# Two of three exponential steps of a chunk moved from tiles 12 to 17 to tiles 18 to 28 of a two-layer transformer kernel

## The chip, the cores and the metric

The kernel runs on one core of one Trainium2 chip. The metric is the device time of one execution in microseconds (us). The kernel before took 1702.78 us in the median of three runs (1702.22 to 1704.12).

## What is computed

Two layers over 32 sequences of 256 tokens with 128 features. Each layer normalises its rows and adds an attention and a mixture of experts to them, all in fp32:

```
x = x + L0_attn(xn) + L0_ffn(xn)        # xn = layernorm(x)
x = x + L1_attn(xn) + L1_ffn(xn)
# L0_attn: linear attention, 16 heads of 8
q_feat = elu(rope(q) * scale) + 1 ;  k_feat = elu(rope(k)) + 1
kv = k_feat^T v ;  den = q_feat . sum(k_feat) ;  out = (q_feat kv / den) W_out
# L0_ffn: 64 experts (8 of them per token, chosen by groups) and a shared one: silu(x Wg) * (x Wu) * coef, times Wd
# L1_attn: 8 best keys per row, softmax over them, and a local message of 4 neighbours with silu
# L1_ffn: 8 experts, 2 per token, gate = softmax(x gate_w)
```

elu(z) + 1 is computed as exp(min(z, 0)) + max(z, 0).

## The kernel before, in words

The tokens are cut into 16 chunks of 512. Layer 0's experts are 33 tiles of 128 hidden columns (32 pairs of experts and the shared one), so TensorE goes through 16 x 33 = 528 tiles, each with three fp32r products for the gate, three for the up half (`first_products`, lines 719 to 721) and the down product of the tile four before (`last_products`: two fp32 passes, line 779, or three fp32r ones, lines 767 to 770, at every fourth tile). Layer 1's expert units follow as another 90 units.

For each tile g, ScalarE computes silu of the gate product (`silu`, L1423) and VectorE multiplies it by the up product (`times_up`, L1003) and, once for two tiles, by the routing coefficients (`times_coef`, L991). There are two PSUM banks for gate products and two for up products: the gate product of tile g waits for silu(g-2), and its up product for times_up(g-2).

Everything else is done beside these tiles, in an order that is written out by hand. The tables `ATTENTION0`, `ROUTE0`, `ROUTE1`, `ATTENTION1` and others give for every step the tile of the chunk at which it is placed; `make_plan` turns them into one list per tile. Each engine runs its instructions in program order, and at every tile g each engine first issues its part of the tile (silu, times_up, products) and then its part of the steps of `plan[g]`, in the tables' order: ATTENTION0, ROUTE0 of the next chunk, ROUTE1 and ATTENTION1 of the chunk before. A step that has not got its operands blocks all that stands behind it on its engine.

The steps that matter here, with their lines:
- `feat_exp` (ScalarE, L1526 and L1528): exp of `k_low` (in the tile mix_a) and of `tmp0`. `q_feat`: relu on ScalarE (L1531), then the sum on GpSimd (L1657). `k_feat` (VectorE, L1127).
- `kvsum` (TensorE, L856), eight products of the features with the values; it waits for k_feat. `kvmask` (VectorE, L1132 and L1134) reads it out. `num0`, `num1` (TensorE, L864) wait for kvmask and for q_feat. `mix0`, `mix1` (VectorE, L1141 to L1145) divide; `mixT` (TensorE, L734, and a copy on ScalarE) transposes.
- `gate_exp` (ScalarE, L1552): exp of layer 1's gate, 32 columns. `attend_exp` (ScalarE, L1561): exp of layer 1's attention scores, at tile 18.
- `near`, `self` (TensorE, three fp32r products each), `p0`, `p1`, `mixa`, `coefT`, `mixl`: other side products. `add1` to `add4`, `mixa_add` (VectorE, L1302), `choice`, `pair4` ... `weigh`: other steps of VectorE.

All side products share three PSUM banks. `make_plan` gives them out in the order of the steps (`free.pop(0)`), and takes a bank back at the step that reads it (`TAKES`). On the chip the next user of a bank waits until the reader before has really finished (`wait_bank`).

exp, silu and sigmoid lie in different activation tables; where ScalarE goes from one to another, the compiler puts an ACT_TABLE_LOAD ahead of the instruction.

The first chunk has a table of its own (`EARLY0`), and chunk 15 has `ROUTE1_LAST`, whose gate_exp is at tile 12. In the text, G(t) is the start of the third gate product (L721) of tile t of chunk 8, which begins at 721.8 us, and silu(t), mul(t) and coef(t) are silu, times_up and times_coef of tile t.

Of the kernel before, what the change touches and what calls it, by code (L numbers as in the profile page):

```python
# [68 lines left out]


ATTENTION0 = [(1, "keys0"), (2, "k_rope"), (4, "q"), (5, "q_copy"), (6, "k_min"), (8, "q_cos"), (9, "q_sin"), (10, "q_min"),
              (12, "feat_exp"), (13, "q_feat"), (14, "k_feat"), (16, "kvsum"), (17, "kvmask"), (19, "num0"), (20, "num1"), (20, "mix0"),
              (24, "mix1"), (26, "mixT")]
FINISH0 = [(4, "yT"), (5, "y_add")]
ROUTE0 = [(0, "stats0"), (2, "norm0"), (4, "xT0"), (5, "x_lo0"), (8, "vr0"), (8, "vr1"), (9, "score"),
          (18, "choice"), (18, "pair4"), (19, "pair2"), (20, "pair1"), (21, "gtop"), (22, "gstrike"), (23, "groups"), (24, "top8"),
          (25, "strike"), (26, "weigh"), (28, "coefT")]

ROUTE0_SECOND = [(at + 6 if at < 10 else at + 1 if at < 14 else at, what) for at, what in ROUTE0]
ROUTE1 = [(5, "stats1"), (7, "norm1"), (8, "xT1"), (9, "x_lo1"), (10, "vl0"), (10, "vl1"), (11, "top1"), (12, "gate_exp"), (23, "softmax"), (30, "select"),  # L80
          (31, "prefix"), (39, "rank"), (40, "key"), (41, "first2"), (42, "slot"), (43, "send0"), (45, "send1"), (47, "send2"), (48, "send3"),
          (49, "send4"), (51, "send5"), (53, "send6"), (54, "send7")]

# [38 lines left out]
def splits1(c):  # L122

    return SPLITS1_FIRST <= c < SPLITS1_FIRST + PARTS1 // SPLITS1_EACH


def make_plan():
# [11 lines left out]
    for g in range(TILES):  # L139
# [3 lines left out]
        steps += [(ROUTE0 if c > 0 else ROUTE0_SECOND, c + 1)] if c + 1 < CHUNKS else []  # L143
        steps += [(ROUTE1 if c < SPARSE else ROUTE1_LAST, c - 1), (ATTENTION1, c - 1)] if c > 0 else [(PREP1, 0)]
        steps += [(SPLITS1, c)] if splits1(c) else []
        plan[g] += [(what, c - 2) for at, what in ROUTE1 if at == j + TILES0 and c > 1]
        plan[g] += [(what, key) for table, key in steps for at, what in table if at == j]
# [1671 lines left out]
```

## Time and profile before

| | |
|---|---|
| median of the runs | 1702.78 us |
| the profiled execution's own time | 1702.63 us |
| its span | 1700.7 us |
| TensorE matmul | 1668.5 us busy (98%) |
| VectorE | 1377.4 us (81%) |
| ScalarE | 877.6 us (52%) |
| GpSimd | 637.5 us (37%) |
| ACT_TABLE_LOAD on ScalarE | 99 of 1.283 us |
| one chunk of 33 tiles in the middle | 88.3 to 88.8 us |

The profile is of one execution on the chip. PE is TensorE, DVE VectorE, ACT ScalarE, POOL GpSimd. In a timeline a row has the start in us, the time it took, engine, line, operation, what it writes and reads, shapes and count; a bracket at its end is the idle time of the engine before it and what ended it. A matmul's end is modelled, and the first product behind an fp32 one is shown early and long; so the third gate product of a tile is the best mark of where TensorE is.

### The profile page before, as it was taken

Reading aid. Unit: us, or ns where it says so; the run is one execution under the profiler, and the core shown is the slowest. Engines: PE = TensorE matmul, PEld = TensorE weight load, DVE = VectorE, ACT = ScalarE, POOL = GpSimd, SP = SyncE. Lnnn points to the kernel's source line nnn. Section 1 sums busy time; section 2 is a strip of 40 time slices with the busy share of each in tenths; the row PEclk is TensorE's granted clock in tenths of the full one; section 3 lists DMA queues with packets and bytes.
Section 4 is the critical chain, followed back from the end, with each engine's and each line's share of the span. In section 5 each row is a group of like instructions: output and inputs, shape, how many; then the busy total and the mean of one; then the engine's idle time right before and its main releaser. Section 6 shows DMA issues by size and latency. Waiting matters only on the chain.

```text
span 1700.7 us, 25018 instructions
## 1 busy us (share of the span) xinstructions
PE 1668.5 (98%) x7158; PEld 1208.5 (71%) x7158; DVE 1377.4 (81%) x3677; ACT 877.6 (52%) x1582; POOL 637.5 (37%) x637
## 2 busy tenths in 40 slices
PE   6999999999999999999999999999999999999997
PEld 4677777777777777777777777777777776767774
DVE  6868888888989797979798888888888887565557
ACT  5546464646464546464555555454646354554432
POOL 4411342424242424333333232333333243567770
PEclk9999999999999999999999999999999999999999
DMA  8858464646374737373737374655546355677758
GB/s 225 195 126 238 116 186 98 186 112 182 99 184 102 180 104 196 97 202 91 196 90 193 87 183 101 160 124 131 152 100 177 91 123 154 211 261 265 239 174 314
DMA packets 172309, 273.92 MB, mean 161 GB/s; under 512 B 14280, under 2 KB 57288, under 8 KB 171920
## 3 DMA queue, kind: packets, MB, share of 16 engines
q1 hardware_dynamic: 163600, 254.63, 56.3%
q0 software_dynamic: 8576, 17.70, 3.3%
q8 instruction: 61, 1.00, 0.3%
q14 instruction: 72, 0.59, 0.1%
HBM read 202.15 MB, written 65.93 MB: 158 GB/s over the span
## 4 chain that ended last, share of the span: by engine, by line
PE 79%; DVE 9%; ACT 6%; issue 4%; DMA 1%; SPq 0%; DVEq 0%; POOL 0%; ACTq 0%; POOLq 0%
PE ps_y L779 17%; PE ps_up L719 7%; PE ps_up L721 7%; PE ps_up L720 7%; PE ps_gate L719 7%; PE ps_gate L721 7%; PE ps_gate L720 7%; PE ps_y L805 4%; PE ps_side L734 3%; DVE silu_h L1003 2%; ACT L1423 1%; DVE silu_h L991 1%; PE ps_side L828 1%; ACT silu_h L1423 1%; ACT L1526 1%
## 5 line engine op out<-in xcount | busy, mean ns | idle before, releaser
L1003 DVE TENSOR_TENSOR silu_h<-ps_up,silu_h 128x512 f32<-128x512 f32 x618 | 421.4, 684 | 267.2 <-ACT silu_h L1423 202.5
L1423 ACT ACTIVATE silu_h<-ps_gate 128x512 f32<-128x512 f32 x618 | 365.9, 598 | 496.0 <-PE ps_gate L721 491.4
L779 PE MATMUL ps_y<-silu_h,w_dn 128*128 128x512 f32 x800 | 407.8, 591 | 1.3 <-DVE silu_h L991 1.3
L991 DVE TENSOR_TENSOR silu_h<-coef_b,silu_h 128x1024 f32<-128x1024 f32 x256 | 321.4, 1256 | 4.4 <-DMA coef_b<-coef_kept 3.2
L719 PE MATMUL ps_gate<-xnT,w_gu 128*128 128x512 f32 x528 | 307.7, 583 | 0.0
L719 PE MATMUL ps_up<-xnT,w_gu 128*128 128x512 f32 x528 | 212.0, 402 | 4.9 <-DVE silu_h L1003 4.6
L721 PE MATMUL ps_gate<-xnT,w_gu 128*128 128x512 f32 x528 | 209.0, 396 | 0.0
L721 PE MATMUL ps_up<-xnT,w_gu 128*128 128x512 f32 x528 | 207.6, 393 | 0.0
L720 PE MATMUL ps_gate<-xnT,w_gu 128*128 128x512 f32 x528 | 206.9, 392 | 0.0
L720 PE MATMUL ps_up<-xnT,w_gu 128*128 128x512 f32 x528 | 206.8, 392 | 0.0
L1705 POOL TENSOR_TENSOR msg<-msg 128x512 f32<-128x512 f32 x48 | 76.7, 1598 | 315.3 <-ACT msg L1586 315.3
L779 PEld LDWEIGHTS ps_y<-silu_h,w_dn 128*128 128x128 f32 x800 | 150.3, 188 | 42.0 <-issue 8.1
L1699 POOL DMA_INDIRECT slots_x<-rows,slot_of x120 | 134.6, 1122 | 110.4 <-PE ps_gate L721 78.3
L1679 POOL DMA_INDIRECT y_kept<-ys,y_to x148 | 143.8, 971 | 59.8 <-issue 48.9
L720 PEld LDWEIGHTS ps_gate<-xnT,w_gu 128*128 128x128 f32 x528 | 100.5, 190 | 54.7 <-issue 48.0
L719 PEld LDWEIGHTS ps_gate<-xnT,w_gu 128*128 128x128 f32 x528 | 100.2, 190 | 54.8 <-issue 46.4
L1638 POOL TENSOR_TENSOR rstd<-rstd,minus_half 128x4 f32<-128x4 f32 x32 | 43.5, 1359 | 244.3 <-DVE shift L1015 244.3
L719 PEld LDWEIGHTS ps_up<-xnT,w_gu 128*128 128x128 f32 x528 | 99.4, 188 | 41.2 <-DVE silu_h L1003 19.8
L721 PEld LDWEIGHTS ps_up<-xnT,w_gu 128*128 128x128 f32 x528 | 99.2, 188 | 23.0
L721 PEld LDWEIGHTS ps_gate<-xnT,w_gu 128*128 128x128 f32 x528 | 99.5, 188 | 22.5
L720 PEld LDWEIGHTS ps_up<-xnT,w_gu 128*128 128x128 f32 x528 | 99.6, 189 | 20.8
L1386 DVE TENSOR_TENSOR h_lo<-silu_h,h_hi 128x512 fp32r<-128x512 f32 x120 | 107.1, 892 | 0.0
(289 smaller groups left out, 2866.7 us busy)
## 6 DMA issues: line engine op xcount, KB each, us to landing
coef_b<-coef_kept SPq DMA_DIRECT2D x254, 512.0 KB, 6.9
slots_x<-empty SPq DMA_DIRECT2D x15, 2080.0 KB, 12.1
w_block<-w_kept SPq DMA_DIRECT2D x45, 512.0 KB, 4.0
xs<-slots_x SPq DMA_DIRECT2D x37, 260.0 KB, 3.8
y_back<-y_kept SPq DMA_DIRECT2D x15, 512.0 KB, 6.8
w_down<-in_ffn_w SPq DMA_DIRECT2D x45, 128.0 KB, 3.8
w_raw<-in_ffn_w SPq DMA_DIRECT2D x33, 128.0 KB, 5.8
xres<-in_x SPq DMA_DIRECT2D x16, 256.0 KB, 2.9
```

What stands on the lines that cost most here:

```text
L719: eng.matmul(dst, w[0], m[0], start=start, stop=False)
L720: eng.matmul(dst, w[1], m[0], start=False, stop=False)
L721: return eng.matmul(dst, w[0], m[1], start=False, stop=stop)
L779: eng.matmul(ps_y[:, :], down_of(j), silu_h[:, h_at(g)], start=j == 0, stop=last).then_inc(pe_down)
L805: eng.matmul(ps_y[:, :], w_down[:, t % BUFS1, f], silu_h[:, h_at(g)], start=first, stop=last).then_inc(pe_down)
L991: eng.tensor_tensor(silu_h[:, s:s + 2], coef_b[:, q % COEF_RING, k:k + 2], silu_h[:, s:s + 2], ALU.mult).then_inc(dve_h)
L1003: eng.tensor_tensor(silu_h[:, s], ps_up[g % 2][:, :], silu_h[:, s], ALU.mult).then_inc(dve_h1)
L1386: eng.tensor_tensor(h_lo[:, :], silu_h[:, h_at(g)], f32(h_hi[:, :]), ALU.subtract).then_inc(dve_hlo)
L1423: eng.activation(silu_h[:, s], ps_gate[g % 2][:, :], ACT.Silu).then_inc(act_silu)
L1679: eng.indirect_dma_start(y_kept, bass.IndirectOffsetOnAxis(y_to[:, c % XPLACES, r:r + 1], 0), ys[:, c % BUFS1, r], None).then_inc(landed[c ...
L1699: eng.indirect_dma_start(slots_x, bass.IndirectOffsetOnAxis(slot_of[:, c % 2, r, k:k + 1], 0), rows1[:, c % 2, r], None).then_inc(sent[c % ...
L1705: eng.tensor_tensor(msg[:, 0], msg[:, 0], msg[:, 1 + k % 2], ALU.add).then_inc(pool_heard)
```

## The change

Only numbers in two tables change. `feat_exp` goes from tile 12 to 18, `q_feat` from 13 to 19, `k_feat` from 14 to 20, `kvsum` from 16 to 21, `kvmask` from 17 to 22, `num0` from 19 to 23, `num1` and `mix0` from 20 to 24, `mix1` from 24 to 26 and `mixT` from 26 to 28, in chunks 1 to 15. `gate_exp` goes from tile 12 to 18 in chunks 1 to 14. `EARLY0`, `ROUTE1_LAST` and `ROUTE1_DENSE` stay as they are. No instruction of the program text is added or removed; the compiler sets the table loads by the new order, and `make_plan` gives out the side banks anew.

```
-              (12, "feat_exp"), (13, "q_feat"), (14, "k_feat"), (16, "kvsum"), (17, "kvmask"), (19, "num0"), (20, "num1"), (20, "mix0"),
-              (24, "mix1"), (26, "mixT")]
+              (18, "feat_exp"), (19, "q_feat"), (20, "k_feat"), (21, "kvsum"), (22, "kvmask"), (23, "num0"), (24, "num1"), (24, "mix0"),
+              (26, "mix1"), (28, "mixT")]
...
-ROUTE1 = [(5, "stats1"), ... (11, "top1"), (12, "gate_exp"), (23, "softmax"), ...
+ROUTE1 = [(5, "stats1"), ... (11, "top1"), (18, "gate_exp"), (23, "softmax"), ...
```

The side banks of a chunk, by the order of the steps (bank numbers 0 to 2, for chunk 8):

| tile | before | after |
|---|---|---|
| 12, 13 | s0 0, s1 2 | s0 0, s1 1 |
| 16, 19, 20 | kvsum 1, num0 0, num1 2 | none |
| 21 | none | kvsum 2 |
| 23 | p0 1, near 0 | num0 0, p0 1, near 2 |
| 24 | p1 1, self 0 | num1 1, p1 2, self 0 |
| 26 | mixT 2, mixa 1 | mixa 2 |
| 28 | coefT 2 | mixT 1, coefT 2 |
| 32 | mixl 1 | mixl 1 |

## Rows read from the trace of the kernel before

**Rows 1.** The page's part 1: busy time, share and instructions of each engine.

```profile
PE 1668.5 (98%) x7158; PEld 1208.5 (71%) x7158; DVE 1377.4 (81%) x3677; ACT 877.6 (52%) x1582; POOL 637.5 (37%) x637
```

**Rows 2.** Waits of PE, 130 to 1480 us, the longest: us in total, times, longest.

```profile
PE ps_up L719 <- DVE silu_h L1003: 3.7, 16, 1.0
```

**Rows 3.** Groups of ACT, by form: table loads (count, busy us, mean ns).

```profile
L1423 ACT ACT_TABLE_LOAD x49 | 62.9, 1283 | 1.0
...
L1526 ACT ACT_TABLE_LOAD x16 | 20.5, 1283 | 0.3
L1561 ACT ACT_TABLE_LOAD x16 | 20.5, 1283 | 0.3
```

**Rows 4.** Timeline of ACT, chunk 8, tiles 12 and 13.

```profile
757.30 1.28 ACT L1526 ACT_TABLE_LOAD   x1
...
761.18 0.60 ACT L1423 ACTIVATE silu_h<-ps_gate 128x512 f32<-128x512 f32 x1
...
762.18 0.63 ACT L1531 ACTIVATE qf<-qf 128x512 f32<-128x512 f32 x1
```

**Rows 5.** Timeline of DVE, tiles 13 and 14: mul(13), h_lo, mul(14).

```profile
761.81 0.69 DVE L1003 TENSOR_TENSOR silu_h<-ps_up,silu_h 128x512 f32<-128x512 f32 x1 [3.14 <-ACT silu_h L1423]
...
763.07 1.66 DVE L1386 TENSOR_TENSOR h_lo<-silu_h,h_hi 128x512 fp32r<-128x512 f32 x1
...
765.79 0.68 DVE L1003 TENSOR_TENSOR silu_h<-ps_up,silu_h 128x512 f32<-128x512 f32 x1
```

**Rows 6.** Timeline of PE, tile 16: G(16), first up product, kvsum.

```profile
765.94 0.40 PE L721 MATMUL ps_gate<-xnT,w_gu 128*128 128x512 f32 x1
766.52 0.50 PE L719 MATMUL ps_up<-xnT,w_gu 128*128 128x512 f32 x1 [0.18 <-DVE silu_h L1003]
...
768.18 1.05 PE L856 MATMUL ps_side<-v,kf 128*128 128x129 f32 x8
```

**Rows 7.** Timeline of ACT, tiles 18 to 20: silu(18), attend_exp, silu(19) and silu(20).

```profile
772.27 0.60 ACT L1423 ACTIVATE silu_h<-ps_gate 128x512 f32<-128x512 f32 x1 [1.12 <-PE ps_gate L721]
...
774.27 1.50 ACT L1561 ACTIVATE scores<-scores,top_neg 128x128 f32<-128x128 f32 x4
...
777.08 1.09 ACT L1423 ACTIVATE silu_h<-ps_gate 128x512 f32<-128x512 f32 x2
```

**Rows 8.** Timeline of POOL, tile 14: the sum of q_feat.

```profile
762.91 1.28 POOL L1657 TENSOR_TENSOR qf<-qf,tmp 128x512 f32<-128x512 f32 x1 [3.91 <-ACT qf L1531]
```

**Rows 9.** Timeline of DVE: k_feat, kvmask, coef(19), mul(21), mul(22), mul(24), mix1, mixa_add, mul(28).

```profile
766.39 0.68 DVE L1127 SCALAR_TENSOR_TENSOR kf<-kf,mix_a 128x512 f32<-128x512 f32 x1
...
772.67 0.91 DVE L1134 TENSOR_SCALAR kv<-att_const,ps_side 128x16 f32<-128x16 f32 x2
...
778.98 1.22 DVE L991 TENSOR_TENSOR silu_h<-coef_b,silu_h 128x1024 f32<-128x1024 f32 x1
...
782.42 0.68 DVE L1003 TENSOR_TENSOR silu_h<-ps_up,silu_h 128x512 f32<-128x512 f32 x1
...
785.80 0.68 DVE L1003 TENSOR_TENSOR silu_h<-ps_up,silu_h 128x512 f32<-128x512 f32 x1
...
790.43 0.68 DVE L1003 TENSOR_TENSOR silu_h<-ps_up,silu_h 128x512 f32<-128x512 f32 x1
...
791.63 0.42 DVE L1145 TENSOR_TENSOR tmp<-ps_side,den_inv 128x256 f32<-128x256 f32 x1
...
799.92 1.13 DVE L1302 SCALAR_TENSOR_TENSOR xres<-ps_side,psum,xres 128x128 f32<-128x128 f32 x4
...
802.70 0.68 DVE L1003 TENSOR_TENSOR silu_h<-ps_up,silu_h 128x512 f32<-128x512 f32 x1
```

**Rows 10.** Timeline of PE: G(21), G(25) and G(29).

```profile
779.31 0.39 PE L721 MATMUL ps_gate<-xnT,w_gu 128*128 128x512 f32 x1
...
790.14 0.39 PE L721 MATMUL ps_gate<-xnT,w_gu 128*128 128x512 f32 x1
...
800.91 0.40 PE L721 MATMUL ps_gate<-xnT,w_gu 128*128 128x512 f32 x1
```

More of the change, by code:

```diff
@@ L79 @@
 ROUTE0_SECOND = [(at + 6 if at < 10 else at + 1 if at < 14 else at, what) for at, what in ROUTE0]
-ROUTE1 = [(5, "stats1"), (7, "norm1"), (8, "xT1"), (9, "x_lo1"), (10, "vl0"), (10, "vl1"), (11, "top1"), (12, "gate_exp"), (23, "softmax"), (30, "select"),
+ROUTE1 = [(5, "stats1"), (7, "norm1"), (8, "xT1"), (9, "x_lo1"), (10, "vl0"), (10, "vl1"), (11, "top1"), (18, "gate_exp"), (23, "softmax"), (30, "select"),
           (31, "prefix"), (39, "rank"), (40, "key"), (41, "first2"), (42, "slot"), (43, "send0"), (45, "send1"), (47, "send2"), (48, "send3"),
```

## The prediction

> **What bounds the kernel now.** I read the shares first: TensorE is busy for 1668.5 of 1700.7 us [rows 1]. Then its waits: from 130 to 1480 us it is held by one thing worth naming, the up product waiting for mul, 3.7 us in 16 waits [rows 2]. So removed work on another engine is worth only what it takes out of such waits, and a new wait on TensorE is paid in full, since nothing behind it has room to catch up. Then the groups of ScalarE: a load of the activation tables takes 1.283 us, and silu, feat_exp and attend_exp cause 49, 16 and 16 of them [rows 3]. Last, the timelines of chunk 8, tile by tile. They show what the waits hide: VectorE, busy for 81%, runs about three us behind TensorE from tile 18 to 30. It is the second bound, and its order matters as much as its sum.
>
> **What goes.** At tile 12 ScalarE loads the exp tables, does two exponentials and the gate's, and loads silu's again: from 757.30 to silu(13) at 761.18, 3.88 us [rows 4]. In chunks 1 to 14 this excursion disappears, for the loads of attend_exp at tile 18 serve all three. That is 14 x 2 = 28 loads x 1.283 = 35.9 us of ScalarE; chunk 15 keeps its gate_exp at tile 12 and its loads. The excursion makes mul(13) wait 3.14 us, h_lo behind it takes 1.66 us since it starts while GpSimd's sum of q_feat runs (762.91 to 764.19), and mul(14) only ends at 766.47 [rows 5, 8]. The up product of tile 16 starts at 766.52, where 765.94 + 0.23 = 766.17 was due, and its first product runs 0.11 longer after the wait [rows 6]: 0.46 us of TensorE. Without the excursion mul(14) is over near 763.6, and this wait is gone: 14 x 0.46 = 6.4 us to the good. That is all that the saved loads are worth directly.
>
> The Trainium skill (ScalarE: Activation LUTs, What ACT_TABLE_LOAD costs) puts a switch at 1283 ns and a drain of some 1380 ns, 2.66 us in all. By it 28 switches would be 74.5 us of ScalarE; the rows have the 1.283 and an exponential right behind it.
>
> **What comes, at tile 21.** kvsum (0.89 us), num0 and num1 (0.49 each) leave tiles 16, 19 and 20, so TensorE gets to tile 21 sooner: from G(16) = 765.94 through four tiles of 2.23 and one of 2.06 it is at G(21) = 776.92, not 779.31 [rows 6, 10]. ScalarE's silu(18) starts at 770.89 (0.49 behind G(18) = 770.40) and ends near 771.5. Then one load (1.28), the two exponentials (0.53 each), the gate's (0.22), attend_exp (1.50, its operands long there) and the load back (1.30): silu(19) runs from 776.89 to 777.49, about as now [rows 7]. The gate product of tile 21 waits for it: G(21) = 777.49 + 0.05 + 0.46 + 0.11 = 778.11, a stall of 1.2 us.
>
> **kvsum behind k_feat.** VectorE sits idle until silu(19), then does mul(19), pair2, coef(19), mul(20) and k_feat. mul(19) at 777.5 puts coef(19) at 778.8. GpSimd's sum of q_feat now starts 0.73 behind the relu (which starts at 777.39), so at 778.12, and lasts to 779.40. By the 1.66 us row coef(19) (1.22 alone) is held to its end and over at 780.5: mul(20) at 780.4, since two neighbours overlap by some 0.1, k_feat 0.6 later at 781.0 (0.68 long), ended at 781.7 [rows 4, 5, 8, 9]. Tile 21's own products end at G(21) + 1.78 = 779.9. kvsum is queued right there and holds tile 22 with it: 1.9 us. With kvsum, G(22) = 783.1, and mul(21) is at 782.4, as it is now.
>
> **num0 behind kvmask.** Between mul(22) and mul(24) VectorE has 1.16 us more, kvmask (0.41 and 0.91, overlapping). It ends at 785.80 + 0.60 + 1.18 = 787.6. TensorE is through with tile 23 at 787.0, so num0 waits 0.7 us, and p0 and near behind it. G(24) = 789.6.
>
> **self behind mix0.** mul(24) comes at 790.43 + 1.16 = 791.6; mix0 follows it in the place where mix1 is now and ends at 791.6 + 1.62 = 793.2 [rows 9]. By the new order of the side banks self takes bank 0 from num0, which mix0 has to have read (now it takes it from near, which ScalarE copies at once). TensorE is there at 792.2: 1.0 us more, plus 0.11, then self. G(25) = 794.5 instead of 790.14, 4.4 us late [rows 10].
>
> **coefT behind mixa_add.** TensorE being late at tile 25, mul(25) can't start before G(25) + 1.15 = 795.7 (now 792.48, 3.2 earlier). mix1 (0.94) is added at tile 26. So mixa_add, which ends at 801.05 now, ends at 805.2, and coefT takes its bank from mixa, where it took mixT's. TensorE is there at 804.6: 0.6 us and 0.11. G(29) = 806.0 instead of 800.91: 5.1 us late (the old stall of tile 16 is already counted in the rows' times). mul(28), now at 802.70, comes at 806.85, only 4.15 later, so the up product of tile 30 no longer waits for it, nor tile 32's: some 0.4 us back. Net 4.7 us a chunk.
>
> Of the Trainium skill one rule speaks of this: gaps that repeat on the engine that should be full can mean too few buffers in SBUF or PSUM (Perfetto Trace Analysis, Optimization Strategy). By that rule alone, with only these two waits for banks, the stalls would be 1.8 us a chunk.
>
> **Moved, at no cost.** The relu and q_feat's sum: num0 is three tiles behind them. mixT's products (0.44) only change tile, and its copy on ScalarE falls where that has room; the copy is wanted in the next chunk's tile 3. GpSimd's scatters are issued at the same tiles; q_feat stood ahead of those of tiles 14 to 16 and now stands ahead of the two of tiles 20 and 21, whose data nobody wants in this chunk. SP issues nothing new, and its queue keeps its order; what it waits for on coefT moves with the chunk. If ScalarE's room at 28 were gone, the copy would be worth 0.6 us.
>
> **The sum.** Chunks 1 to 14: 14 x 4.7 = 65.8. Chunk 15 has no routing behind it, but layer 1's tables; the same steps by its own timeline give 3.0 us. Chunk 0 and layer 1's units do not change. 1702.6 + 68.8 = 1771.4 for the profiled execution, 0.15 below the median; I say 1770. Two prices are not in the trace. Whether GpSimd holds coef(19) like h_lo: nothing or 0.6 us a chunk, I take 0.6, same pair of engines, same kind of operands. Whether restarts after each stall add up: 0.11 each, 0 to 0.3 a chunk, I take 0.2 since VectorE's chain absorbs those upstream. All the stalls hang on one another; an error of 1.5 us a chunk is possible, 21 us either way.
>
> **Rivals.**
> (a) *Faster.* TensorE is the bound and loses only the wait of tile 16: 1702.6 - 6.4 = 1696, at best 1690 with tiles 30 and 32. It decides at tile 21: silu(19) would have to be over by 776.4 and k_feat by 779.9, so TensorE would have to come as late as it does now. Against it: side products of 1.87 us have left the tiles ahead. The Trainium skill (ScalarE: Activation LUTs, Rules for kernel authors) wants the calls of one table set done together before switching, which is this mechanism.
> (b) *Slower, but mildly.* No cascade: VectorE never waits for TensorE after mul(19). It has 24.99 us between mul(19) and mul(28) now, and 0.6 + 1.16 more then, so mul(28) is 1.6 (2.2 with the hold) late and TensorE pays 1.2 to 1.8 a chunk: 1720 to 1728. With self's wait but not coefT's, 1750. For it: VectorE's other waits are short. Against: mul(25) has two us of idle ahead of it in my working, because self is late.
> (c) *No change*: the new stalls just cancel the old, 0.46 + 0.4 a chunk. That needs every one of five to be near nothing.
>
> **Numbers.** The forecast (1745 and more) has 0.72, (b) below 1745 has 0.15, (c) 0.04, (a) 0.09. The range leaves out (a), (c) and most of (b): 1735 to 1790. What differs by less than 0.2% (3.4 us) can't be told from no change. Slower 0.87, same 0.04, faster 0.09.
>
> **What would show it.** Loads: 35 at silu, 16 at feat_exp, one at attend_exp, two at gate_exp. In a middle chunk of 93 us, where it was 88.5: the up product of tile 16 without a wait; a gate product waiting for silu once a chunk (tile 21); kvsum waiting for k_feat, num0 for kvmask, self for mix0, coefT for mixa_add. TensorE's granted clock as before. I am wrong if chunks stay under 89.5 us, or if kvsum finds k_feat done.

## The result, and the profile after

The kernel after took 1779.83 us in the median of five runs (1778.67 to 1780.20). On the same chip the kernel before took 1702.93 (1702.22 to 1704.25). The ratio is 1.0441, with a 95% interval of 1.0429 to 1.0452: 4.4% slower. The profiled execution has a span of 1777.9 us.

Part 1 of the page, to be read against [rows 1]:

```profile
PE 1688.7 (95%) x7158; PEld 1221.7 (69%) x7158; DVE 1388.2 (78%) x3677; ACT 841.5 (47%) x1554; POOL 624.6 (35%) x637
```

ScalarE has 28 instructions and 36.1 us less: the saving that was to be had is there in full. The span is 77.2 us longer all the same, and TensorE itself is busy 20.2 us longer with the same 7158 products. The groups of ScalarE say where the loads went, against [rows 3]:

```profile
L1423 ACT ACT_TABLE_LOAD x35 | 44.9, 1283 | 1.1 <-PE ps_gate L721 0.4
L1526 ACT ACT_TABLE_LOAD x16 | 20.5, 1283 | 0.3
L1552 ACT ACT_TABLE_LOAD x2 | 2.6, 1283 | 0.0
L1561 ACT ACT_TABLE_LOAD x1 | 1.3, 1283 | 0.0
```

The waits of TensorE, 130 to 1560 us (us in total, times, longest), are where the loss is named. Before, one entry of 3.7 us led this list [rows 2]; it is gone, and four others stand there:

```profile
PE ps_side L856 <- DVE kf L1127: 35.7, 15, 2.4
PE ps_gate L719 <- ACT silu_h L1423: 12.1, 14, 0.9
PE ps_side L834 <- DVE xres L1302: 7.3, 14, 0.5
PE ps_side L719 <- DVE tmp L1145: 5.8, 9, 0.7
```

That is kvsum waiting for k_feat, the gate product of tile 21 for silu(19), coefT for the bank of mixa, and self for the bank of num0. Two chunks of the kernel after, in windows that meet their bounds within 0.1 us (length, busy time and count of each engine, granted clock as a share of 2.4 GHz, DMA share, GB/s), the first of them chunk 8, the second chunk 9:

```profile
758.60:852.90 94.30, 90.38 (x386) 66.36 (x384) 77.75 (x213) 45.59 (x85) 30.23 (x31) 0.98 0.53 136
852.90:946.20 93.30, 88.79 (x383) 64.87 (x383) 77.34 (x213) 45.59 (x85) 30.02 (x31) 1.00 0.53 137
```

And chunk 8 of the kernel before:

```profile
721.79:810.54 88.75, 88.53 (x385) 64.73 (x384) 76.70 (x213) 48.16 (x87) 29.84 (x31) 1.00 0.57 145
```

TensorE stood still for 88.75 - 88.53 = 0.22 us of chunk 8 before. The chunks before are not all alike (88.3 to 88.8 us), so those of after are compared with the mean of chunks 1 to 14, which is 1239.6 / 14 = 88.54 us: 0.2 of standing still and 88.3 of products. In chunk 9 after, TensorE stands still for 4.51 us, and its products take 0.5 more than in the mean. In chunk 8 after it stands still for 3.92, but its products take 2.0 more, and the clock column reads 0.98: part of this chunk ran at the lower level. So there are two kinds of chunk after, and nearly the whole difference is made of them.

Now the place itself, chunk 8 from tile 18 on. ScalarE, with silu(18), the one excursion to the exp tables (first exponential of feat_exp, attend_exp), the load back, silu(19), and the relu of q_feat:

```profile
807.71 0.60 ACT L1423 ACTIVATE silu_h<-ps_gate 128x512 f32<-128x512 f32 x1 [1.14 <-PE ps_gate L721]
808.33 1.28 ACT L1526 ACT_TABLE_LOAD   x1
809.62 0.63 ACT L1526 ACTIVATE mix_a<-mix_a 128x512 f32<-128x512 f32 x1
...
810.80 1.48 ACT L1561 ACTIVATE scores<-scores,top_neg 128x128 f32<-128x128 f32 x4
812.30 1.28 ACT L1423 ACT_TABLE_LOAD   x1
813.59 0.60 ACT L1423 ACTIVATE silu_h<-ps_gate 128x512 f32<-128x512 f32 x1
814.09 0.62 ACT L1531 ACTIVATE qf<-qf 128x512 f32<-128x512 f32 x1
```

VectorE in the same stretch: mul(19), the first operation of pair2, coef(19), mul(20), k_feat, and later mul(22) and kvmask:

```profile
814.22 0.69 DVE L1003 TENSOR_TENSOR silu_h<-ps_up,silu_h 128x512 f32<-128x512 f32 x1 [3.25 <-ACT silu_h L1423]
814.83 1.34 DVE L1049 TENSOR_TENSOR coef<-struck 128x64 f32<-128x64 f32 x1
...
816.67 1.22 DVE L991 TENSOR_TENSOR silu_h<-coef_b,silu_h 128x1024 f32<-128x1024 f32 x1
817.81 0.69 DVE L1003 TENSOR_TENSOR silu_h<-ps_up,silu_h 128x512 f32<-128x512 f32 x1
818.41 0.68 DVE L1127 SCALAR_TENSOR_TENSOR kf<-kf,mix_a 128x512 f32<-128x512 f32 x1
...
823.45 0.69 DVE L1003 TENSOR_TENSOR silu_h<-ps_up,silu_h 128x512 f32<-128x512 f32 x1 [0.22 <-PE ps_up L721]
...
824.39 0.37 DVE L1134 TENSOR_SCALAR kv<-att_const,ps_side 128x16 f32<-128x16 f32 x2
```

GpSimd's sum of q_feat, and the products of TensorE that met a wait (gate of tile 21, kvsum, coefT) with G(22) and G(29):

```profile
814.80 1.28 POOL L1657 TENSOR_TENSOR qf<-qf,tmp 128x512 f32<-128x512 f32 x1 [5.56 <-ACT qf L1531]
```

```profile
814.33 0.47 PE L719 MATMUL ps_gate<-xnT,w_gu 128*128 128x512 f32 x1 [0.86 <-ACT silu_h L1423]
...
819.24 1.61 PE L856 MATMUL ps_side<-v,kf 128*128 128x129 f32 x8 [2.40 <-DVE kf L1127]
821.50 0.63 PE L721 MATMUL ps_gate<-xnT,w_gu 128*128 128x512 f32 x1
...
843.00 0.44 PE L834 MATMUL ps_side<-common,coef 128*128 128x128 f32 x2 [0.53 <-DVE xres L1302]
843.75 0.39 PE L721 MATMUL ps_gate<-xnT,w_gu 128*128 128x512 f32 x1
```

VectorE stands idle for 3.25 us in front of mul(19), because silu(19) sits behind the excursion (about the 3.14 us that it stood idle at tile 12 [rows 5], but now with TensorE right behind it). Everything it owes TensorE comes behind that in its fixed order, and k_feat is fifth. kvsum, queued on TensorE since 816.84, gets its operand at 819.09. Chunk 8 starts 36.8 us later than before; with that taken off, G(29) is at 806.95, where it was at 800.91 [rows 10].

The third gate product of tile 22 takes 0.63 us there instead of 0.39. The windows say why: just before kvsum, TensorE is idle; just behind, its granted clock is at half, 1.2 GHz; then full again.

```profile
817.00:819.00 2.00, 0.00 (x0) 0.00 (x0) 2.00 (x3) 0.62 (x1) 1.42 (x2) 1.00 0.10 33
820.00:823.00 3.00, 3.00 (x10) 2.52 (x10) 2.97 (x12) 0.60 (x1) 0.00 (x0) 0.50 0.96 271
824.00:829.00 5.00, 5.00 (x26) 4.21 (x25) 4.68 (x23) 2.09 (x4) 0.00 (x0) 1.00 0.03 7
```

In chunk 9 the same place has the same idle time and stays at full clock:

```profile
911.00:913.00 2.00, 0.08 (x1) 0.00 (x0) 2.00 (x4) 0.62 (x1) 1.67 (x2) 1.00 0.10 33
914.00:917.00 3.00, 3.00 (x16) 2.23 (x15) 2.96 (x13) 0.60 (x1) 0.00 (x0) 1.00 1.04 271
```

The same three microseconds hold 16 products in the one and 10 in the other. Chunks 1 to 15 have eight such stretches of 3.4 us, each right behind a kvsum that had waited; before there were none.

### The profile page after: what moved, and what is told of

The parts are those of the page before. It is cut to its first block, busy times and chain, and to the rows that moved or that the text cites. A ratio compares the mean times of both kernels' runs of the same rounds, so it can differ in the third digit from the quotient of the medians.

```text
span 1777.9 us, 24990 instructions
## 1 busy us (share of the span) xinstructions
PE 1688.7 (95%) x7158; PEld 1221.7 (69%) x7158; DVE 1388.2 (78%) x3677; ACT 841.5 (47%) x1554; POOL 624.6 (35%) x637
## 4 chain that ended last, share of the span: by engine, by line
PE 72%; DVE 17%; ACT 6%; issue 4%; DMA 1%; SPq 0%; DVEq 0%; POOL 0%; ACTq 0%; POOLq 0%
PE ps_y L779 14%; PE ps_gate L719 6%; PE ps_gate L721 6%; PE ps_gate L720 6%; PE ps_up L719 6%; PE ps_up L721 6%; PE ps_up L720 6%; PE ps_y L805 4%; DVE silu_h L1003 4%; DVE silu_h L991 3%; PE ps_side L734 2%; PE ps_side L828 1%; ACT silu_h L1423 1%; PE ps_side L905 1%; ACT L1423 1%
## 5 line engine op out<-in xcount | busy, mean ns | idle before, releaser
L991 DVE TENSOR_TENSOR silu_h<-coef_b,silu_h 128x1024 f32<-128x1024 f32 x256 | 329.1, 1286 | 4.7 <-DMA coef_b<-coef_kept 3.5
L1705 POOL TENSOR_TENSOR msg<-msg 128x512 f32<-128x512 f32 x48 | 65.5, 1364 | 362.6 <-ACT msg L1586 362.6
L1679 POOL DMA_INDIRECT y_kept<-ys,y_to x148 | 141.9, 959 | 60.9 <-issue 49.8
L719 PEld LDWEIGHTS ps_gate<-xnT,w_gu 128*128 128x128 f32 x528 | 101.5, 192 | 79.4 <-issue 71.9
L720 PEld LDWEIGHTS ps_gate<-xnT,w_gu 128*128 128x128 f32 x528 | 101.7, 193 | 55.3 <-issue 47.9
L719 PEld LDWEIGHTS ps_up<-xnT,w_gu 128*128 128x128 f32 x528 | 100.8, 191 | 27.3 <-DVE silu_h L1003 3.4
L721 PEld LDWEIGHTS ps_up<-xnT,w_gu 128*128 128x128 f32 x528 | 100.5, 190 | 23.1
L721 PEld LDWEIGHTS ps_gate<-xnT,w_gu 128*128 128x128 f32 x528 | 100.7, 191 | 22.7
L720 PEld LDWEIGHTS ps_up<-xnT,w_gu 128*128 128x128 f32 x528 | 100.9, 191 | 22.2
L805 PE MATMUL ps_y<-silu_h,w_down 128*128 128x512 f32 x180 | 92.0, 593 | 2.5 <-DVE silu_h L997 1.7
```

The lines of the kernel that those rows point to most:

```text
L719: eng.matmul(dst, w[0], m[0], start=start, stop=False)
L720: eng.matmul(dst, w[1], m[0], start=False, stop=False)
L721: return eng.matmul(dst, w[0], m[1], start=False, stop=stop)
L805: eng.matmul(ps_y[:, :], w_down[:, t % BUFS1, f], silu_h[:, h_at(g)], start=first, stop=last).then_inc(pe_down)
L991: eng.tensor_tensor(silu_h[:, s:s + 2], coef_b[:, q % COEF_RING, k:k + 2], silu_h[:, s:s + 2], ALU.mult).then_inc(dve_h)
L1679: eng.indirect_dma_start(y_kept, bass.IndirectOffsetOnAxis(y_to[:, c % XPLACES, r:r + 1], 0), ys[:, c % BUFS1, r], None).then_inc(landed[c ...
```

## The experiments

The theory to be tested had four parts: the saved loads are worth only tile 16's wait; the loss comes from where silu(19) and the products of VectorE fall, not from the loads; the fixed order carries it on to kvsum; and two waits for banks add to it. The rivals: the excursion's own length costs the time, or TensorE waits for something else at that place that changes with the order. All stretches below are measured the same way, from the start of the first gate product of chunk 1 to that of chunk 15. "Half" counts the stretches at the lower clock in chunks 1 to 15.

| kernel | time, ratio to before | chunks 1 to 14 | half |
|---|---|---|---|
| before | 1702.93 | 1239.6 | 0 |
| after | 1779.83, 1.0441 | 1314.0 | 8 |
| e1 copies for exponentials in before | 1741.58, 0.9943 | 1234.5 | 0 |
| e2 only gate_exp to 18 | 1751.47, 0.9998 | 1241.4 | 0 |
| e3 after, k_feat at 19 | 1818.62, 1.0381 | 1306.8 | 1 |
| e4 after, exponentials cut short | 1815.44, 1.0362 | 1301.8 | 7 |
| e5 after, routing ahead of mul(19) | 1754.11, 1.0292 | 1287.7 | 1 |
| e6 before, q_feat at 15 | 1705.34, 1.0008 | 1242.3 | 0 |
| e7 before, routing at 12 | 1698.60, 0.9969 | 1235.9 | 0 |
| e8 e6 and e7 together | 1699.65, 0.9975 | 1237.1 | 0 |
| e9 after, mixT at 27 | 1771.96, 1.0383 | 1307.2 | 8 |
| e10 after, q_feat at 22 | 1759.14, 1.0318 | 1292.7 | 0 |
| e11 e8 and layer 1's parts later | 1698.84, 0.9961 | 1236.2 | 0 |
| e12 after's grouping, placed anew | 1722.87, 1.0107 | 1259.3 | 0 |

e1 to e4 ran on a chip on which the kernel before itself took 1752.37 us, with layer 1's part some 45 to 54 us longer in the profiles of all four. There is no profile of the kernel before on that chip; e2, whose ratio is 1, has its chunks there as before has them elsewhere (1241.4 us against 1239.6). So times of e1 to e4 are read as ratios, and between groups of runs the chunk stretch is compared. Before took 1704.37 beside e5 to e8, and 1705.48 beside e9 to e12.

### e1: what the excursion at tile 12 is worth

```
-  eng.activation(k_low[:, :], k_low[:, :], ACT.Exp)       # feat_exp; tmp0 likewise
+  eng.activation(k_low[:, :], k_low[:, :], ACT.Copy)
-  eng.activation(gate[:, :, :], gate[:, :, :], ACT.Exp)   # gate_exp
+  eng.activation(gate[:, :, :], gate[:, :, :], ACT.Copy)
```

> The kernel before, with the exponentials of feat_exp and gate_exp replaced by plain copies in place (left out: the exponentials of layer 0's features and of layer 1's gate). Their time on ScalarE stays, their table loads go: 30 and more loads of 1.283 us. Theory (only the wait of tile 16's up product is worth something): 14 x 0.46 = 6.4 us less, 1696.5 us. Rival (a load on ScalarE is paid by the kernel): about 38 us less, 1664 us. If neither the wait nor the loads matter: 1702.9.

Measured: 0.9943 [0.9928, 0.9957]; chunks 1 to 14 are 5.1 us shorter. The wait at tile 16 is off the list, and no other has come into it in the chunks; the trace has one small thing in its place, a first up product of tile 32 that takes 0.50 us instead of 0.39 in 13 of the 14 chunks. The excursion at tile 12, loads and all, costs 5.1 us in 14 chunks; 6.4 had been reckoned. The whole kernel is 7.5 to 12.6 us shorter; where the rest comes from can't be said without a profile of before on that chip. That the saved loads lie on the way to the end, which would be 38 us, is ruled out either way.

### e2: the gate's exponential alone

```
-ROUTE1 = [..., (12, "gate_exp"), ...
+ROUTE1 = [..., (18, "gate_exp"), ...
```

> The kernel before with gate_exp alone at tile 18. No load is saved; the excursion at tile 12 is 0.22 us shorter, the one at tile 18 0.22 longer. Theory: mul(14) comes 0.22 us sooner, so half of tile 16's wait of 0.46 goes; silu(19) has 1.07 us to spare and costs nothing: 14 x 0.22 = 3 us less, 1700 us. Rival (tile 18's excursion is already at its limit): 3 us more, 1706.

Measured: 0.9998 [0.9984, 1.0013], chunks 1241.4: nothing. The wait of tile 16 shrank by 0.11 us (16 such waits of 3.7 us in the list of before are now 2 of 1.1), and yet the chunks are no shorter, and the 3 us that I expected did not come. The trace shows where they went: TensorE stands still 1.4 us less in chunks 1 to 14, but is busy 3.2 us longer. In e2 the first up products of tiles 30 and 32 take 0.50 us in every one of these chunks, which I read as a mul that ends just too late for them. In before that of tile 30 does so in 7 chunks (0.44 to 0.45 in the rest) and that of tile 32 in 6 (0.39 in the rest). Whether the edit or the chip does this isn't shown. This part of the change is neutral, so the loss lies in layer 0's steps.

### e3: k_feat one tile earlier in the kernel after

```
-  (19, "q_feat"), (20, "k_feat"), (21, "kvsum"),
+  (19, "q_feat"), (19, "k_feat"), (21, "kvsum"),
```

> The changed kernel with k_feat at tile 19, ahead of pair2 and coef(19). Theory (VectorE's order from mul(19) on carries the loss; the single waits hang on one another): kvsum's wait of 2.4 us shrinks to about 0.1, but num0 now waits some 1.5 us for kvmask and self still for mix0, so that only 0.9 us a chunk comes back, and with it the stretches at half clock: 14 x 0.9 + 6 = 18 us less than the changed kernel, 1761 us. Rival (each wait is paid on its own): 15 x 2.6 + 6 = 45 us less, 1735 us.

Measured: 1.0381 [1.0361, 1.0402], chunks 1306.8. The waits of TensorE, 130 to 1580 us:

```profile
PE ps_side L864 <- issue: 22.9, 15, 1.9
PE ps_gate L719 <- ACT silu_h L1423: 12.2, 14, 0.9
PE ps_side L719 <- DVE tmp L1145: 10.0, 14, 0.7
...
PE ps_up L719 <- DVE silu_h L1003: 7.3, 15, 0.5
```

kvsum's wait of 2.4 us is gone, and 1.5 us a chunk stand at num0 (L864; 1.9 in chunk 15), 0.5 at the up products and 0.7 at self. num0 of chunk 8 starts at 821.69 us, kvmask ends at 821.59 and q_feat's sum at 813.28, so it is kvmask that num0 waits for. What was taken from one wait came back in the others: 0.9 us a chunk had been expected, but chunks at full clock take 93.3 us as before the edit; the 7 us less are the seven stretches at half clock that did not occur. GpSimd's sum, too, only found another instruction to hold: k_feat, which starts at 812.03 and takes 1.80 us instead of 0.68, beside the sum from 812.00 to 813.28. Which wait gets the time is decided by the order; how much there is, is decided by VectorE, whose order holds the same work between mul(19) and mul(24).

### e4: the exponentials at tile 18 cut short

```
-  eng.activation(k_low[:, :], k_low[:, :], ACT.Exp)         # tmp0 likewise
+  eng.activation(k_low[:, 0:8], k_low[:, 0:8], ACT.Copy)
-  eng.activation(gate[:, :, :], gate[:, :, :], ACT.Exp)
+  eng.activation(gate[:, :, :], gate[:, :, :], ACT.Copy)
```

> The changed kernel with feat_exp done as copies of 8 columns and gate_exp as a copy (left out: the exponentials of the features and of the gate), so that the excursion at tile 18 is some 0.8 us shorter. Theory: the gate product of tile 21 waits 0.8 us less, the rest of the chain moves along with mul(19), and kvsum still waits 2.4 us for k_feat: 15 x 0.8 = 12 us less, 1768 us. Rival (the length of the excursion does not matter, the waits for VectorE do it alone): no change, 1780.

Measured: 1.0362 [1.0342, 1.0382], chunks 1301.8, which is 12.2 less; 12 had been said. The wait of the gate product is gone, that of kvsum is not:

```profile
PE ps_side L856 <- DVE kf L1127: 35.4, 15, 2.4
```

The excursion is shorter by 0.86 us (VectorE's idle time ahead of mul(19) is 2.39 in chunk 8, where it was 3.25), and this length is worth its 0.87 us a chunk at tile 21 and no more. The larger part of the loss is not in the length of the exponentials. That silu(19) comes late behind the excursion stays so in this run, so e4 says nothing against that.

### e5: fill VectorE's idle time ahead of mul(19)

```
-  (18, "choice"), (18, "pair4"), (19, "pair2"), (20, "pair1"), (21, "gtop"), (22, "gstrike"), (23, "groups"),
+  (18, "choice"), (18, "pair4"), (18, "pair2"), (18, "pair1"), (18, "gtop"), (18, "gstrike"), (18, "groups"),
```

(In this kernel, and in e7, e8, e11 and e12, chunk 0 keeps the old places; lines lie 2 further on.)

> The changed kernel with pair2, pair1, gtop, gstrike and groups all at tile 18 (chunk 0 as it was), so that VectorE does them in its idle 3.2 us ahead of mul(19). Theory (the loss is in VectorE's order behind a late mul(19)): k_feat comes 0.7 us sooner, kvsum waits some 1.7 us instead of 2.4, the half-clock stretches go, self waits less; coefT's wait stays. Chunks 1 to 14 take 1314 - 22 = 1292 us. Rival (the waits come from where the feature steps stand, whatever VectorE does beside them): 1307 us, as with k_feat at tile 19.

Measured: 1.0292 [1.0277, 1.0308], chunks 1287.7, 26.3 less. TensorE's waits, 130 to 1580 us:

```profile
PE ps_side L858 <- DVE kf L1129: 22.5, 15, 2.1
PE ps_gate L721 <- ACT silu_h L1425: 12.5, 15, 0.9
PE ps_side L836 <- DVE xres L1304: 7.3, 14, 0.5
PE ps_side L721 <- DVE tmp L1147: 0.8, 2, 0.5
```

The five routing steps that stood behind mul(19) now run while VectorE waits for silu(19) anyway. kvsum's wait falls from 35.7 to 22.5 us, self's nearly vanishes, and with them all but one stretch at half clock. This is the direct evidence that the order on VectorE, with the 3.25 us that it stands idle, carries a good part of the loss: 26.3 us here, some 6 of them clock.

### e6, e7, e8, e11: versions of the kernel before

First, does GpSimd's sum hold what VectorE runs beside it? e6 moves it off h_lo:

```
-  (12, "feat_exp"), (13, "q_feat"), (14, "k_feat"),
+  (12, "feat_exp"), (15, "q_feat"), (14, "k_feat"),
```

> The kernel before with q_feat at tile 15 instead of 13 and nothing else. Theory (half of the delay behind the wait of tile 16 is GpSimd's sum holding h_lo for 1.0 us): mul(14) ends 1.0 us sooner, the wait goes, chunks 1 to 14 take 1239.6 - 6.4 = 1233 us. Rival (h_lo is late by silu(13) alone, or the hold only moves to k_feat): 1239 to 1241 us.

Measured: 1.0008 [0.9998, 1.0017], chunks 1242.3. The wait of tile 16 is gone but another has come, and the waits of TensorE read:

```profile
PE ps_side L856 <- DVE kf L1127: 3.3, 8, 0.4
PE ps_up L719 <- DVE silu_h L1003: 1.0, 1, 1.0
```

In 8 chunks kvsum now waits, as the rival had it; e8 below shows which instruction the sum holds there. e7 makes VectorE's work at tiles 18 to 20 less by using its 3.14 us of idle time at tile 12 [rows 5]:

```
-  (18, "choice"), (18, "pair4"), (19, "pair2"), (20, "pair1"),
+  (12, "choice"), (12, "pair4"), (12, "pair2"), (12, "pair1"),
```

> The kernel before with choice, pair4, pair2 and pair1 at tile 12 (chunk 0 as it was), done in the 3.1 us in which VectorE waits for silu(13). Theory (VectorE runs full from tile 18 to 30, and tiles 30 and 32 wait for it): 2.4 us less of its work lies there, and these waits of 0.4 us go; tile 16's stays: 1239.6 - 5.6 = 1234 us. Rival (what mul(28) waits for is not VectorE's queue): 1239 to 1241 us.

Measured: 0.9969 [0.9956, 0.9983], chunks 1235.9: 3.7 less, where 5.6 had been said; the kernel as a whole is 2.9 to 7.5 us faster. The wait of tile 16 stays in the list; the chunks that had taken 88.4 to 88.8 us now take 88.25 like the rest. The trace names the products: in chunk 8 before, the first up products of tiles 30 and 32 take 0.51 us, in e7 0.39 in every chunk. So VectorE, with less work behind tile 18, is no longer late for them. e8 takes both edits:

> The kernel before with both edits, q_feat at tile 15 and the four routing steps at tile 12. Theory: all of TensorE's small waits in chunks 1 to 14 are gone: 1239.6 - 12 = 1228 us there, 12 us less than the kernel before in all (0.7%). Rival (one wait takes the other's place): 1234 us or more.

Measured: 0.9975 [0.9966, 0.9984], chunks 1237.1 where 1228 had been expected. From chunk 10 on they take 87.79 us with TensorE never idle, but chunks 2 to 9 take 88.7, with kvsum waiting again. VectorE and GpSimd in chunk 8 show k_feat:

```profile
766.82 2.21 DVE L1129 SCALAR_TENSOR_TENSOR kf<-kf,mix_a 128x512 f32<-128x512 f32 x1
```

```profile
764.20 1.02 POOL L1634 TENSOR_TENSOR part_split<-part_raw,part_split 128x256 fp32r<-128x256 f32 x1
765.43 1.73 POOL L1701 DMA_INDIRECT slots_x<-rows,slot_of  x1 [0.21 <-PE ps_gate L723]
767.19 1.29 POOL L1659 TENSOR_TENSOR qf<-qf,tmp 128x512 f32<-128x512 f32 x1
```

k_feat takes 2.21 us instead of the 0.68 of [rows 9]: it starts while the scatter (L1701) still runs and ends behind the sum that follows. In these chunks `part0` of layer 1 (L1634) stands ahead of that scatter in GpSimd's queue. In chunk 12, without it, the scatter is over at 1119.68 and the sum starts at 1119.70, and k_feat, from 1119.35, takes 0.68 as when alone. So e11 moves layer 1's parts back:

```
-SPLITS1 = [(14, "part0"), (16, "part1")]
+SPLITS1 = [(22, "part0"), (24, "part1")]
```

> The kernel before with q_feat at tile 15, choice to pair1 at tile 12, and part0 and part1 (the weight splits of chunks 2 to 9, GpSimd) at tiles 22 and 24 instead of 14 and 16. Theory (with both edits alone q_feat's sum stood behind a split, held k_feat and made kvsum wait in just these chunks): every chunk takes 87.8 us as the later ones did, chunks 1 to 14 take 1229.5 us, 10 us less than the kernel before. Rival (the splits hold something at tiles 22 to 24 instead): 1236 us.

Measured: 0.9961 [0.9947, 0.9975], chunks 1236.2. Chunk 8 and a late chunk in windows:

```profile
721.12:809.78 88.66, 88.35 (x385) 64.80 (x384) 76.21 (x213) 48.08 (x87) 29.41 (x31) 1.00 0.56 145
986.59:1074.38 87.79, 87.79 (x386) 64.98 (x384) 76.32 (x214) 47.67 (x85) 28.27 (x29) 1.00 0.55 138
```

The wait at kvsum is gone, and in its place the up products of tile 30, and in most of these chunks of tile 32, wait in chunks 2 to 9, as the rival had it. What holds VectorE there is in the trace: in each of chunks 2 to 9 one times_coef takes 1.76 or 1.77 us instead of 1.22 (in chunk 8 from 782.15, while `part0` runs on GpSimd from 781.90 to 782.82); in chunks 10 to 14, which have no part, it takes 1.22, and nothing waits. The late chunk, with its length and TensorE's busy time equal to the hundredth, is the floor that this order could reach. Both e7 and e11 beat both kernels, by 0.31% and 0.39%; their intervals overlap, so which is the better stays open.

### e9: one bank free earlier

```
-  (26, "mix1"), (28, "mixT")]
+  (26, "mix1"), (27, "mixT")]
```

> The changed kernel with mixT at tile 27 instead of 28; coefT then takes its bank from mixT, which ScalarE reads at once, and not from mixa. Theory (the waits behind kvsum's are paid by themselves, since VectorE waits for TensorE from tile 22 on): the wait of 0.53 us and its restart of 0.11 go: 14 x 0.64 = 9 us, chunks 1 to 14 take 1305 us. Rival (the up product of tile 30 then waits for mul(28) instead): 1314 us.

Measured: 1.0383 [1.0366, 1.0400], chunks 1307.2, 6.8 less where 9 had been said and the rival said nothing. coefT's wait is off the list (7.3 us before), kvsum's is at 35.8, and the half-clock stretches are still eight. The wait for the bank is real, worth what the list gives for it, and stands apart from the others.

### e10: the sum away from the chain

```
-  (18, "feat_exp"), (19, "q_feat"), (20, "k_feat"), (21, "kvsum"),
+  (18, "feat_exp"), (22, "q_feat"), (20, "k_feat"), (21, "kvsum"),
```

> The changed kernel with q_feat at tile 22 instead of 19. Theory (GpSimd's sum holds pair2 for 1.1 us, and TensorE idle for 2.4 us is what brings the half clock): k_feat comes 1.1 us sooner, kvsum waits 1.3 us, no half-clock stretch in the middle chunks: 14 x 1.5 = 22 us less, chunks 1 to 14 take 1292 us. Rival (the clock falls by the sum of the waits, whichever they are): 1298 us, with half-clock stretches left.

Measured: 1.0318 [1.0302, 1.0334], chunks 1292.7; 1292 had been said. The waits, 130 to 1580 us:

```profile
PE ps_side L856 <- DVE kf L1127: 18.5, 15, 1.3
PE ps_gate L719 <- ACT silu_h L1423: 12.5, 15, 0.9
PE ps_side L719 <- DVE tmp L1145: 10.9, 15, 1.0
PE ps_side L834 <- DVE xres L1302: 7.2, 14, 0.5
```

kvsum's wait falls by (35.7 - 18.5) / 15 = 1.15 us a chunk, what pair2's first operation had been held for (1.34 - 0.21 = 1.13), and no stretch at half clock is left. Self's wait of 0.7 us now comes in all the chunks, where it came in about half of them, and the chunk takes 92.3 us.

### e12: the grouping, placed as well as I could

```
-  (19, "q_feat"), (20, "k_feat"), (21, "kvsum"), (22, "kvmask"), (23, "num0"), (24, "num1"), (24, "mix0"),
-  (26, "mix1"), (28, "mixT")]
+  (21, "q_feat"), (20, "k_feat"), (22, "kvsum"), (23, "kvmask"), (24, "num0"), (25, "num1"), (25, "mix0"),
+  (26, "mix1"), (29, "mixT")]
```

and the line of e5.

> The changed kernel's grouping of exponentials at tile 18, with the rest placed where VectorE can serve it: pair2 to groups at tile 18, k_feat 20, q_feat 21, kvsum 22, kvmask 23, num0 24, num1 and mix0 25, mix1 26, mixT 29. Theory (the loss is in where the products stand, the grouping itself costs only the gate product of tile 21 waiting for silu(19)): a chunk takes 87.8 + 1.2 = 89.0 us, chunks 1 to 14 take 1246 us, 6 us more than the kernel before. Rival (VectorE's idle time before mul(19) is lost in any case and comes back as waits at tiles 22 to 30): 1270 us or more.

Measured: 1.0107 [1.0092, 1.0122], chunks 1259.3, between theory (1246) and rival (1270 and more). The waits of kvsum, self and coefT are all gone; the gate product of tile 21 still waits:

```profile
PE ps_gate L721 <- ACT silu_h L1425: 12.5, 15, 0.9
```

Of the 74.4 us that the chunks had gained, 54.7 hang on where the steps were put (some 6 of them clock), and 19.7 are left with the excursion grouped and this order. TensorE stands still for 12.5 of them, 12.2 at this wait in chunks 1 to 14, and is busy for the other 7.2: the first up products of tiles 21, 30 and 32, for instance, take 0.50 us instead of 0.39 in most chunks. With its 28 loads saved the grouped kernel is still slower than the kernel before.

## Why the prediction was right

The forecast was 1770, the range 1735 to 1790, the result 1779.83, and the case named as likeliest is the one that occurred. By its steps:

- **What goes** (6.4 us to the good). Right in kind: the up product of tile 16 no longer waits, and e1 gives 5.1 us for the same excursion in the chunks. The loads' 35.9 us bought nothing else. The table loads came out as named, 35, 16, 1 and 2.
- **Tile 21** (wait of 1.2 with the restart). The list has 0.86 and the product runs some 0.1 longer. G(21) of chunk 8, less the 36.8, is at 778.08; 778.11 was said.
- **kvsum** (1.9). It waits 2.40. The step that was mis-sized is the hold by GpSimd: I let it fall on coef(19) and took 0.6. It fell on pair2's first operation, which takes 1.34 us instead of 0.21, so 1.1 (e10 confirms the size: 1.15 less in the wait).
- **num0** (0.7). Did not occur. kvmask's L1134 takes 0.37 here, not the 0.91 of [rows 9], and TensorE, later by the longer wait ahead, finds it done. This and the step before nearly cancel. In e3, where kvsum no longer waits, the wait at num0 appears at once.
- **self** (1.1). 0.7 us in chunks at full clock and 0.1 in chunk 8: TensorE is later than in my working, so less is left to wait.
- **coefT** (0.7). 0.53 and a slower start. The size is right, and e9 takes it away alone.
- **The sum.** In chunk 9, at full clock, TensorE's idle time is 4.51 us, which the four waits (2.4 + 0.86 + 0.7 + 0.53 = 4.49) explain to 0.02. Against the mean chunk of before that is 4.3 more, and 0.5 more busy (first products behind a wait are slower, about 0.1 us each; this is part of it): 4.8 a chunk, where 4.7 had been predicted. Two wrong terms cancelled; the total is not evidence for each of them.
- **"TensorE's granted clock as before"**. Wrong, and most of what the forecast is short by. The seven chunks with a half-clock stretch take some 0.9 us more each, 6 to 7 us in all. Chunks 1 to 14: 14 x 4.8 + 7 x 0.9 = 73.5, against 74.4 measured. Chunk 15 gave 3.0 as predicted, but by luck: a stretch at half clock is in it, which the 3.0 did not have.

The rivals: *faster* falls with e1 (the removed excursion is worth 5 us) and with kvsum's wait. *Mildly slower* needed VectorE never to wait for TensorE behind mul(19). In chunk 9, at full clock, it stands idle for 2.00 us ahead of mul(25) (926.78 us), which waits for silu(25) and so for the gate product that self's wait had delayed: the two us of idle time that the prediction held against this rival. In chunk 8 the half clock makes TensorE late earlier, and mul(22) waits 0.22 us. And e5, which only gives VectorE more room, returns 26 us. *No change* falls with the list: 60.9 us of new waits. The Trainium skill's advice to do the calls of one table set together (ScalarE: Activation LUTs, Rules for kernel authors) holds here for ScalarE's own time, 36.1 us less, and not for the kernel's: e12, the best placement tried with it, is 1.1% slower than the kernel before.

Left open: why a wait of 2.4 us is followed by the half clock in only about every second chunk; whether it is the edit or the chip that makes TensorE wait at tiles 30 and 32 in every chunk of e2; and what all of the 7 us of longer busy time of e12 are made of. Another order of VectorE for the grouped exponentials, with silu(19) ahead of the excursion, wasn't tried.

## What to carry to other kernels

A saved instruction is worth the waits of the bounding engine that it ends; read those before counting loads. When work leaves one place on an engine that runs full, that engine reaches the next place earlier, and whatever stood just in time there (here silu(19), then k_feat, then two PSUM banks) becomes a wait; so ask for each moved step which idle time it leaves behind on the second engine, and put that engine's free work there. Merging two excursions makes one longer one: check who stands behind it.

## What was not expected of the hardware

**A GpSimd sum and a VectorE operation hold each other, whole.** Two VectorE operations that started just behind the start of GpSimd's sum of two SBUF tiles ended just behind its end: pair2's first by 0.09 us (814.83 to 816.17, the sum from 814.80 to 816.08; 1.34 us instead of 0.21), and k_feat in e3 by 0.55 (812.03 to 813.83, the sum until 813.28; 1.80 instead of 0.68). k_feat in e8 had started 0.37 us ahead of the sum, while a scatter of GpSimd ran, and ended 0.55 behind the sum (769.03 and 768.48; 2.21 instead of 0.68). A 128x64 operation is held as fully as a 128x512 one. It goes the other way too: in chunk 8 of e10 times_coef runs from 811.29 to 812.51 in its usual 1.22 us, and the sum, shown from 811.64, takes 2.03 us instead of 1.28. times_up, which reads one of its inputs from PSUM, starts at 812.43 inside that sum and takes its usual 0.68. The Trainium skill says that GpSimd shares its SBUF interface with VectorE and that operations with two SBUF inputs contend (GPSIMD Engine Reference, Specifications); by that rule, the traces agree for these cases, with a price of 1.1 us for pair2's operation and in e3, and of 1.5 us in e8.

**The clock of TensorE.** In after, e4 and e9 the longest wait of each of chunks 1 to 14 is 2.3 to 2.4 us, and half clock (1.2 GHz) followed it in 7 of the 14, in each of the three kernels. In chunk 15 it followed longest waits of 1.90 (e3), 2.09 (after) and 2.10 us (e5, e9), and did not follow 1.81 (e4) and 2.04 (e10). Where the longest wait was 1.6 us or less (chunks 1 to 14 of e3, e5, e10 and e12) it never came. So a wait of this length can cost 0.9 us more than it lasts, and whether it does isn't settled by its length alone.

**A restart.** The first product behind a wait runs about 0.1 us longer than in a row of products (0.50 us instead of 0.39 at tile 16 [rows 6]). Busy time of TensorE, 88.53 us in chunk 8 before, is 87.79 in e11's chunks without a wait and 88.8 in chunk 9 of after: busy time is no constant of the work.
